# One copy of q and k in DRAM, read back by strided loads

## The reference

```
q, k, v = x @ Wq.T + bq, x @ Wk.T + bk, x @ Wv.T + bv        # per head 512 x 16
p = softmax(q k^T / sqrt(512)), then p * triu(ones)          # mask after the softmax
a = layernorm(x + p v) * gamma + beta
x2 = layernorm(x + a)
h = silu(x2 W1^T s1) * (x2 W2^T s2)                          # 1024 wide
h = gelu(h H1^T t1); h = gelu(h H2^T t2); y = h W3^T s3
out = layernorm(x2 + y)
```

## Time and profile before

| | us |
|---|---|
| median of 3 runs | 1239.02 |
| lowest and highest | 1238.99, 1242.73 |
| the profiled execution | 1233.03 |
| its span, from the first to the last instruction | 1231.2 |
| PE busy in the span | 1169.1 (95%) |
| mean granted clock of PE | 0.973 of full |
| DMA traffic | 128.48 MB, mean 104 GB/s |

### The profile page before, as it was taken

The page is one execution under the profiler, slowest core; times in us unless marked ns, Lnnn a source line. Parts: engine busy times, 40 slices in busy tenths (PEclk is TensorE's granted clock), DMA queues, the critical chain, the costliest instruction groups (busy, mean ns, idle before and its releaser), DMA issues.

```text
span 1231.2 us, 18365 instructions
## 1 busy us (share of the span) xinstructions
PE 1169.1 (95%) x7430; PEld 815.6 (66%) x7430; DVE 785.5 (64%) x1135; ACT 526.2 (43%) x698; POOL 590.7 (48%) x502
## 2 busy tenths in 40 slices
PE   4379999999999999999999999999999999999997
PEld 2134777758776677857777587766778577775886
DVE  3657677477646686477774777466864777748412
ACT  5777411564127621375115641276213751155310
POOL 5867532465235642376324652355423763246432
PEclk8569999999999999999999999999999999999999
DMA  9973631425334343246414263343432454141000
GB/s 339 285 197 67 190 86 36 123 70 172 70 88 105 138 103 70 53 105 187 87 36 122 64 178 70 88 106 137 103 71 53 105 181 89 41 96 46 1 1 18
DMA packets 55451, 128.48 MB, mean 104 GB/s; under 512 B 4032, under 2 KB 15680, under 8 KB 53312
## 3 DMA queue, kind: packets, MB, share of 16 engines
q1 hardware_dynamic: 51008, 115.44, 36.5%
q10 hardware_dynamic: 4352, 11.80, 2.9%
HBM read 88.95 MB, written 38.27 MB: 103 GB/s over the span
## 4 chain that ended last, share of the span: by engine, by line
PE 87%; POOL 4%; DMA 4%; issue 3%; ACT 1%; DVE 1%; POOLq 0%; ACTq 0%; SPq 0%; DVEq 0%
PE PS L1018 51%; PE PS L935 9%; PE PS L954 6%; PE PS L903 6%; PE PS L855 5%; PE PS L1104 3%; PE PS L961 3%; PE PS L872 2%; PE PS L967 2%; DMA raw_weights<-h2T_dram 1%; POOL raw_weights L520 1%; POOL diag_probs L453 1%; DMA x_tok<-x_dram 1%; DMA raw_weights<-h1T_dram 1%; DVE out_tok L711 1%
## 5 line engine op out<-in xcount | busy, mean ns | idle before, releaser
L665 DVE TENSOR_REDUCE neg_max<-PS 128x3 f32<-128x1536 f32 x168 | 257.6, 1575 | 61.1 <-PE PS L903 61.1
L440 POOL TENSOR_TENSOR hidA_lo<-hidA_full,hidA_hi 128x512 fp32r<-128x512 f32 x128 | 174.1, 1360 | 244.7 <-DVE hidA_hi L822 186.8
L575 ACT ACTIVATE probsT<-PS 128x1024 f32<-128x1024 f32 x256 | 248.0, 1021 | 76.8 <-PE PS L935 76.7
L1018 PE MATMUL PS<-hidA_hi,g 128*128 128x512 f32 x512 | 205.7, 402 | 0.0
L1018 PE MATMUL PS<-hidC_hi,g 128*128 128x512 f32 x512 | 204.1, 399 | 0.0
L1018 PE MATMUL PS<-hidA_lo,g 128*128 128x512 f32 x512 | 200.1, 391 | 0.0
L1018 PE MATMUL PS<-hidC_lo,g 128*128 128x512 f32 x512 | 200.0, 391 | 0.0
L453 POOL TENSOR_TENSOR diag_probs<-probsT,mask 128x512 f32<-128x512 f32 x120 | 157.3, 1315 | 57.4 <-PE PS L1018 31.1
L440 POOL TENSOR_TENSOR hidC_lo<-hidC_full,hidC_hi 128x512 fp32r<-128x512 f32 x64 | 82.3, 1286 | 194.5 <-DVE hidC_hi L822 194.5
L935 PE MATMUL PS<-stacks 66*128 66x512 f32 x512 | 152.3, 419 | 0.2 <-ACT probsT L575 0.2
L596 ACT ACTIVATE hidC_full<-PS,scales 128x512 f32<-128x512 f32 x64 | 44.1, 690 | 239.3 <-PE PS L1018 239.3
(11 more groups left out here) (106 smaller groups left out, 1805.3 us busy)
## 6 DMA issues: line engine op xcount, KB each, us to landing
stacks<-qk_rows SPq DMA_DIRECT2D x64, 512.0 KB
stacks<-qk_rows SPq DMA_DIRECT2D x32, 1024.0 KB
qk_rows<-qk_hi SPq DMA_DIRECT2D x32, 512.0 KB, 3.7
qk_rows<-qk_lo SPq DMA_DIRECT2D x32, 512.0 KB, 5.6
xT_sb<-xT_dram SPq DMA_DIRECT2D x8, 512.0 KB, 4.0
raw_weights<-h1T_dram ACTq DMA_DIRECT2D x8, 512.0 KB, 9.8
raw_weights<-h2T_dram ACTq DMA_DIRECT2D x8, 512.0 KB, 8.3
x_tok<-x_dram SPq DMA_DIRECT2D x8, 512.0 KB, 5.7
```

What stands on the lines that cost most here:

```text
L440: nc.gpsimd.tensor_tensor(lo[:, m, :], full[:, m, :], hi[:, m, :], ALU.subtract).then_inc(lo_done, 1)
L575: nc.scalar.activation(PT[:, s % RING, 2 * pair:2 * pair + 2, :], PS[:, 2 * pair:2 * pair + 2, :], ACT.Exp, scale=SCALE).then_inc(exp_done, 1)
L665: nc.vector.tensor_reduce(NEGM[:, group // 2, at + lo:at + hi], PS[:, 3 * side:3 * side + hi - lo, :], AX.X, ALU.max, negate=True).then_in ...
L1018: ins = nc.tensor.matmul(out, d if swapped else w, w if swapped else d, start=(k == 0 and part == 0), stop=(k == kts - 1 and part == 1))
```

## The change

`qk_rows` holds q and k once. Its axes are now q or k, group, side (which half of the four heads), dimension, hi or lo, and two heads x 512, so one row is 4 KB: both heads of a side for one dimension and one part. The weights' columns are put into another order on the host (`pairs_outside`), so that a tile's partitions are group, side, dimension, and the tile is the head of the pair. Four stores of 512 KB remain.

The rows of a stack become: partition 4d + 2 (q's part) + (k's part), plus 64 per side in the loads for the row scores. q's rows, being wanted twice, are loaded with a partition stride of 2 by two DMAs; each of k's parts is loaded with a stride of 4 by two DMAs. A load for the row scores is 2 DMAs of 64 rows and 4 of 32, over all 128 partitions; a transposed load is 2 of 32 rows and 4 of 16, over partitions 0 to 63, and the one of the maxima. In `ST` the q values of the four heads now lie ahead of the k values. The counts on the semaphores follow. Loading, rounding and testing the weights stay.

```diff
--- before.py
+++ after.py
@@ -104,7 +104,7 @@
 
     XT = place("xT_sb", [P, DT, S], F32)
     ZB = place("z_blocks", [P, HD, 2 * HD], F32)
-    ST, ST_f = both("stacks", [P, 2, QUAD, 2, S])
+    ST, ST_f = both("stacks", [P, 2, 2, QUAD, S])
     VXT = place("v_ones", [P, QT * VX + HD], F32)
     X = place("x_tok", [P, QT, D], F32)
     Vm = place("v_negative", [P, QT, D], F32, top[0])
@@ -139,7 +139,7 @@
     UNBOUNDED = place("scores_unbounded", [1, 1], I32)
     assert top[0] <= nc.sbuf_usable_end, top[0] - nc.sbuf_usable_end
 
-    qk_rows = nc.dram_tensor("qk_rows", [4, D, 2, S], F32, kind="Internal").ap()
+    qk_rows = nc.dram_tensor("qk_rows", [2, NQUAD, 2, HD, 2, 2 * S], F32, kind="Internal").ap()
     max_rows = nc.dram_tensor("max_rows_d", [2, H * QT * P], F32, kind="Internal").ap()
 
     with ExitStack() as ctx:
@@ -205,7 +205,7 @@
             if value > 0:
                 engine.wait_ge(s, value)
 
-        LOADS_S, LOADS_T = 32, 32
+        LOADS_S, LOADS_T = 6 * 16, 7 * 16
         IN_PER_BATCH = 2 * LOADS_S + 2 * LOADS_T
 
         def after_stack(engine, b, group, transposed):
@@ -283,6 +283,15 @@
             sp.dma_start(ID[:], ident).then_inc(consts_in, 16)
             for t, src in ((GAM, gamma), (BET, beta), (S3, s3)):
                 sp.dma_start(t[:], src.rearrange("(a d) -> a d", a=1).to_broadcast([P, D])).then_inc(consts_in, 16)
+
+            def load_rows(stack, group, landed):
+
+                for r1 in range(2):
+                    sp.dma_start(stack(slice(r1, P, 2))[:, 0:2, :].rearrange("m pair s -> m (pair s)"),
+                                 qk_rows[0, group].rearrange("side d part e -> (side d part) e")).then_inc(landed, 16)
+                    for r2 in range(2):
+                        sp.dma_start(stack(slice(2 * r1 + r2, P, 4))[:, 2:4, :].rearrange("m pair s -> m (pair s)"),
+                                     qk_rows[1, group, :, :, r2, :].rearrange("side d e -> (side d) e")).then_inc(landed, 16)
 
             def load_stacks(b, group, transposed):
 
@@ -298,31 +307,33 @@
                 else:
                     after(sp, scoredT, b, n, back)
                 if group == 0 and not transposed:
-                    after(sp, rows_stored, b, 8 * 16, 8 * 16)
-                rows = qk_rows.rearrange("r (d h) a s -> (r d) h a s", d=HD)
+                    after(sp, rows_stored, b, 4 * 16, 4 * 16)
                 if not transposed:
-                    for side in range(2):
-                        heads = group * QUAD + 2 * side
-                        sp.dma_start(ST_f[side * SPLIT:(side + 1) * SPLIT, group % 2, :, 0, :],
-                                     rows[:, heads:heads + 2, :, :].rearrange("p h a s -> p (h a) s")).then_inc(
+                    load_rows(lambda rows: ST_f[rows, group % 2, 0, :, :], group, stack_in[group % 2])
+                else:
+                    for r2 in range(2):
+                        sp.dma_start(ST_f[r2:SPLIT:2, group % 2, 0, :, :].rearrange("m (side pair) s -> m side (pair s)", pair=2),
+                                     qk_rows[0, group].rearrange("side d part e -> (d part) side e")).then_inc(
                                          stack_in[group % 2], 16)
-                else:
-                    sp.dma_start(ST_f[0:SPLIT, group % 2, :, :, :],
-                                 rows[:, group * QUAD:(group + 1) * QUAD, :, :]).then_inc(stack_in[group % 2], 16)
+                    for r1 in range(2):
+                        for r2 in range(2):
+                            sp.dma_start(ST_f[2 * r1 + r2:SPLIT:4, group % 2, 1, :, :].rearrange(
+                                "d (side pair) s -> d side (pair s)", pair=2),
+                                         qk_rows[1, group, :, :, r2, :].rearrange("side d e -> d side e")).then_inc(
+                                             stack_in[group % 2], 16)
                     if group % 2 == 0:
                         after(sp, max_stored, b, 32, 16 * (group // 2 + 1))
-                    sp.dma_start(ST_f[SPLIT:ROWS, group % 2, :, 0, :],
+                    sp.dma_start(ST_f[SPLIT:ROWS, group % 2, 0, :, :],
                                  max_rows[:, group * QUAD * S:(group + 1) * QUAD * S].rearrange(
                                      "r (h s) -> r h s", h=QUAD)).then_inc(stack_in[group % 2], 16)
 
             def store_rows(b):
 
-                for part, done, products in ((QKhi_f, qk_biased, ((0, 1), (0, 2))), (QKlo_f, qk_split, ((2, 3), (1, 3)))):
+                for part, values, done in ((0, QKhi_f, qk_biased), (1, QKlo_f, qk_split)):
                     for a in range(2):
                         after(sp, done, b, 2 * DT, (a + 1) * DT)
-                        for r in products[a]:
-                            sp.dma_start(qk_rows[r, :, a, :].rearrange("(t p) s -> p t s", p=P),
-                                         part[:, a * DT:(a + 1) * DT, :]).then_inc(rows_stored, 16)
+                        sp.dma_start(qk_rows[a].rearrange("g side d part (pair s) -> part (g side d) pair s", pair=2)[part],
+                                     values[:, a * DT:(a + 1) * DT, :]).then_inc(rows_stored, 16)
 
             def chunks(b, first, count, source):
 
@@ -420,7 +431,7 @@
             sp.wait_ge(out_ready, QT * B)
             sp.dma_start(out[(B - 1) * S:B * S, :].rearrange("(t p) d -> p t d", p=P), OUT[:]).then_inc(out_stored, 16)
             sp.wait_ge(out_stored, 16 * B)
-            sp.wait_ge(rows_stored, 8 * 16 * B)
+            sp.wait_ge(rows_stored, 4 * 16 * B)
             sp.wait_ge(max_stored, 2 * 16 * B)
 
 
@@ -624,7 +635,7 @@
         @block.vector
         def _(dve):
             nc.vector.memset(ONESF[:], 1.0).then_inc(consts_set, 1)
-            nc.vector.memset(ST_f[SPLIT:ROWS, :, :, 1, :], 1.0).then_inc(consts_set, 1)
+            nc.vector.memset(ST_f[SPLIT:ROWS, :, 1, :, :], 1.0).then_inc(consts_set, 1)
             nc.vector.memset(VXT[:], 1.0).then_inc(consts_set, 1)
             nc.vector.memset(NEGM[:], 0.0).then_inc(consts_set, 1)
             nc.vector.memset(HALF[:], -0.5).then_inc(consts_set, 1)
@@ -802,7 +813,7 @@
                         after(dve, qk_split, b, 2 * DT, 4 * DT)
                     if m == 4 and not last:
                         sum_squares(b + 1)
-                        after(dve, rows_stored, b, 8 * 16, 16 * 16)
+                        after(dve, rows_stored, b, 4 * 16, 8 * 16)
                     nc.vector.scalar_tensor_tensor(out=hidA_full[:, m, :], in0=PS[:, bank1(m, 1), :],
                                                    scalar=SC[:, 1, m:m + 1], in1=SIL[:, m % 2, :],
                                                    op0=ALU.mult, op1=ALU.mult).then_inc(up_done, 1)
@@ -901,8 +912,8 @@
                     for side in range(2):
                         rows = slice(side * SPLIT, (side + 1) * SPLIT)
                         ins = nc.tensor.matmul(PS[:, base + apart * side + n, :],
-                                               ST[rows, group % 2, 2 * pair, 0, qt * P:(qt + 1) * P],
-                                               ST[rows, group % 2, 2 * pair + 1, 0, :],
+                                               ST[rows, group % 2, 0, pair, qt * P:(qt + 1) * P],
+                                               ST[rows, group % 2, 0, 2 + pair, :],
                                                start=True, stop=True)
                 ins.then_inc(scored, 1)
 
@@ -932,8 +943,8 @@
                         after(pe, max_split, b, 2, 2)
                         after_units(pe, maxed, b, 2 * units_of(b), 2)
                     for j in (2 * pair, 2 * pair + 1):
-                        ins = nc.tensor.matmul(PS[:, j, :], ST[0:ROWS, g % 2, j, 1, kt * P:(kt + 1) * P],
-                                               ST[0:ROWS, g % 2, j, 0, :], start=True, stop=True)
+                        ins = nc.tensor.matmul(PS[:, j, :], ST[0:ROWS, g % 2, 1, j, kt * P:(kt + 1) * P],
+                                               ST[0:ROWS, g % 2, 0, j, :], start=True, stop=True)
                     ins.then_inc(scoredT, 1)
 
             def values(b, s):
@@ -1163,10 +1174,10 @@
     def turned(w):
         return np.ascontiguousarray(np.asarray(w).T)
 
-    def dim_major(w):
+    def pairs_outside(w):
 
         w = np.asarray(w)
-        return w.reshape(H, HD, *w.shape[1:]).swapaxes(0, 1).reshape(w.shape)
+        return np.moveaxis(w.reshape(NQUAD, 2, 2, HD, *w.shape[1:]), 2, 0).reshape(w.shape)
 
     def by_partition(*vectors):
 
@@ -1175,8 +1186,8 @@
     arrays = {
         "x": np.ascontiguousarray(x.reshape(B * S, D)),
         "xT": np.ascontiguousarray(x.transpose(0, 2, 1).reshape(B * D, S)),
-        "wqT": turned(dim_major(L0_attn_Wq)), "wkT": turned(dim_major(L0_attn_Wk)), "wvT": turned(L0_attn_Wv),
-        "bqk": by_partition(dim_major(L0_attn_bq), dim_major(L0_attn_bk)), "bv": np.asarray(L0_attn_bv),
```

(2 more changed lines are left out.)

## The result

Ten runs of each kernel on one chip: 1230.41 us with the change (1227.12 to 1233.33), 1238.84 us before (1235.11 to 1242.73). The ratio, taken between runs made next to each other, is 0.9941, interval 0.9921 to 0.996: **7.3 us faster, with about 2.4 us either way** (the two medians alone differ by 8.4). Forecast were 1234.3 us and a gain of 4.7. The profiled executions differ by less: 1229.9 against 1233.03 us, a gain of 3.1 (span 1228.2 against 1231.2). Written to DRAM were 21.50 MB instead of 38.27.

A forecast was written before the change was run, and what follows sets the result against it. The first 82 us were taken as bound by weight starvation (7.1 us) and row maxima, PE as full later. -7.1 + 0.9 stall + 1.5 clock = -4.7 took 1239.0 to 1234.3 us, range 1228.5 to 1240.

The forecast's parts named there:

- Stores, 5.3 us: Startup, batch 0: halving the stores lets the first stack load leave SP at 22.5 us, 5.3 us earlier.
- The rate of strided loads, 380 to 400 GB/s: Row-score loads: strided over all 128 partitions, they move 380 to 400 GB/s, within possible bounds of 217 and 407.
- rival 1: Row-score loads: strided loads stay at the half rate, only the stores' part helps; gain 2.1, 1236.9 us; chance 0.22.
- The weights, 7.1 us of starvation gone, 0.9 kept: First 82 us: late weight pieces cost 7.1 us, which goes; 0.9 us of stall stays beside group 0's transposed load.
- The clock, 1.5 us: Startup, PE idle from about 73 to 75.5 us: its lowered clock costs 1.5 us, bounds 0 and 2.5.
- The startup's sum, -4.7 us: Startup: -7.1 weight starvation + 0.9 stall + 1.5 clock loss = -4.7 us, bounds -7.1 and -2.1.
- x_tok being late in each batch: Later batches, kernel before: five more late x_tok at 1.1 us explain nearly all of the median's 6 us above the profile.
- x_tok and the transposed loads, 0 us: SP queue, group 2: seven issues instead of one just fit before x_tok; cost 0, bounds -2.3 and +9.5 us.
- the sign that I had named for rival 3: SP queue: x_tok's issue held up by SP's own issues, listed among the signs that the forecast is wrong.
- rival 3: SP's queue behind the group 2 load: x_tok late in every batch, +4.8 us, 1243.8 us; chance 0.13.
- Rival 2: Startup and late batches: the whole gain comes and x is relieved, -7.1 - 2.3 = -9.4, 1229.6 us; chance 0.15.

The follow-up runs named there:

- experiment 7: Changed kernel with each q and k store issued twice, the second time into a spare array (eight stores again): 1231.44 us, ratio 0.9949.
- Experiments 8 and 9: Changed kernel, each row-score load cut in two, reaching 64 partitions (8, by side) or all 128 (9, by parity): 1238.04 and 1230.8 us.
- by parity: Experiment 9: changed kernel, twelve row-score DMAs a group, each over all 128 partitions with strides of 4 and 8: 1230.8 us, ratio 0.9949.
- experiments 7 and 11: 7: changed kernel, every store issued twice, 1231.44 us; 11: changed kernel, w3T pieces third among the weights instead of last, 1232.06 us.
- experiment 10: Changed kernel with sixteen instead of two clock-keeping matmuls on PE before the first exp: 1229.08 us, ratio 0.9944.
- x early: Experiments 5 and 6: x_tok loaded into its own buffer ahead of the group 2 load; kernel before 1232.07 us, changed kernel 1225.22 us.
- loads by side: Experiment 8: changed kernel, twelve row-score DMAs a group, each over 64 partitions: 1238.04 us, ratio 0.9998.
- experiments 1 and 2: Only the first two batches computed, the other six left out: kernel before 372.03 us, changed kernel 369.64 us.

## Why the prediction was right, and where it was not

The time fell into the range in part by luck: two errors of opposite sign met in it, as the sum below shows.

**Stores, 5.3 us: right.** The first load came at 22.39 for a forecast of 22.5, and experiment 7 gave 5.8 us back.

**The rate of strided loads, 380 to 400 GB/s: right**, 400 in SP's own queue. It was the disputed step, with rival 1 on its other side. Experiments 8 and 9 have the same number of DMAs with equally few rows in each, and differ in the partitions that a DMA reaches: 235 GB/s over 64, 290 over 128. The Trainium skill, in "SBUF — State Buffer", section "Door 1: The DMA port swizzle", has the rate go by the ports that a transfer's partitions reach. Strides of 2 and 4 over 128 partitions at 400 GB/s against 231 to 235 over 64 agree with it. By its formula a stride of 8, which half of the bytes by parity have, reaches eight of the 16 ports again; half at 400 and half at 231 would give 293 GB/s, an estimate from that page and these rows, and measured were 290. No run separates the stride of 8 from the smaller DMAs. The Trainium skill has a rule to coalesce small transfers ("DMA: Bandwidth & Descriptors", section "Rules for kernel authors"); going against it cost no time here: 512 KB DMAs became 256 and 128 KB, and even 128 and 64 KB in experiment 9, and 1230.8 us stood beside 1230.41.

**The weights, 7.1 us of starvation gone, 0.9 kept: mechanism right, the rest mis-sized.** The median piece of h1T lands 5.8 us after its issue instead of 9.8, and h1T and h2T are never waited for. (The prediction misread one row: the piece of 9.99 us was issued at 34.80 and landed at 44.79. Nothing in the sum hangs on it.) But the stall that I kept for the transposed load, 0.9 us, is 2.1 us at POOL and 2.7 at ScalarE; experiments 7 and 11 point to that load. The maxima ended 1.2 us later than forecast, at 71.75, since the first ones started at 31.47 and not at 29 to 30: PE took up the first group at 30.2, and I had it landed at 28.3. The first exp came 4.5 us earlier, not 6.2: POOL's stall is 1.2 us above the 0.9, and the pieces' work itself ran 0.4 us later (29.04 instead of 28.61). My upper bound for that stall was 2.5 us: the size should have been taken from the earlier trace rows, where the same overlap had left POOL idle for 2.50 us, and nothing in the change touches that load's reach. This and the clock are the two terms that were mis-sized.

**The clock, 1.5 us: mechanism right, size too small.** It took 3.1 us between the first exp and the stores of batch 1, 2.4 of which experiment 10 gets back. I had sized it from the earlier trace rows, where half clock lasts some 3 us behind an idle time of about 2.4 us; here PE was idle for 4.17 us and the half clock lasted from 76 us to past 86. One row of another gap was too little to size it by.

**The startup's sum, -4.7 us.** In the profiled pair it is -4.5 + 3.1 = -1.4, and -2.7 with the clock's fall of the old kernel at 126 us. The timed runs give 2.4 by the two batches and 6.85 by the pair with x early, with some 2 and 4 us of uncertainty. The traces say why the profiled pair can be low. In the seven other profiled executions that keep four stores and row-score loads over all 128 partitions, the first exp starts between 74.52 and 77.69, in six of them at 76.36 or later. Of the old startup, it was 81.65 in the execution that I predicted from, and 82.56 and 83.77 in two others; with the loads by side 82.88. The one I had was the best of these, so a gain worked out from it is small against that of the median. That is read from few traces. The forecast came within 3.9 us of the time with two errors of opposite sign: too large a gain against its own profile (by 1.6), too small a one against the timed runs (by 2.6).

**Where the old kernel's 6 us above its profile are.** I put nearly all on x_tok being late in each batch. That step was wrong. x early gives 5.9 us in the median, but the profiled execution had nearly all of that loss itself: from the stores of batch 2 to the end of the span it took 1231.2 - 273.41 = 957.8 us, and 1226.7 - 274.00 = 952.7 with x early, 5.1 us less. The two late batches are only part of it; the other periods are 0.2 us longer than 143.24 as well, and the last batch 1.7. So x accounts for about 0.8 of the 5.8 us between profile and median. The rest lies in other differences between executions ("What stays open", below).

**x_tok and the transposed loads, 0 us: right, in another way.** I had the seven issues at 0.45 us, 3.2 together. SP's queue in batch 1:

```profile
233.45 1.24 SPq L315 DMA_DIRECT2D stacks<-qk_rows  x2
234.72 2.50 SPq L320 DMA_DIRECT2D stacks<-qk_rows  x4
237.27 0.44 SPq L326 DMA_DIRECT2D stacks<-max_rows_d  x1
237.75 1.02 SPq L408 DMA_DIRECT2D x_tok<-x_dram  x1
```

and its DMA issues by line (ns, least, median, most), beside the earlier trace rows:

```profile
L293 SPq DMA_DIRECT2D stacks<-qk_rows x128: 448/596/1221, 23.0 to 1039.6; - x128
L320 SPq DMA_DIRECT2D stacks<-qk_rows x128: 557/593/607, 59.6 to 1107.3; - x128
L290 SPq DMA_DIRECT2D stacks<-qk_rows x64: 456/592/1549, 22.4 to 1038.3; - x64
L315 SPq DMA_DIRECT2D stacks<-qk_rows x64: 592/601/1436, 58.3 to 1104.8; - x64
```

An issue of the transposed load costs 0.59 to 0.60 us, and all seven with x behind them 4.3 us. So x_tok leaves at 237.75, 0.44 us after VectorE's last output tile (237.31) and held by SP itself: the sign that I had named for rival 3. It didn't matter, because x waits for the data ahead of it, not for its issue. From the first issue of the group 2 load to the landing of x it is 9.64 us in the mean of seven batches before and 9.68 after. With the change x was late twice, in the last two batches, where it landed 10.0 and 10.6 us after that issue. The rows of the last one (landed at 1105.3):

```profile
1099.54 0.41 SPq L408 DMA_DIRECT2D x_tok<-x_dram  x1
...
1105.33 1.01 DVE L731 TENSOR_TENSOR z<-z,x_tok 128x256 f32<-128x256 f32 x1 [2.78 <-DMA x_tok<-x_dram]
...
1109.31 0.42 PE L965 MATMUL PS<-probsT,ones_col 128*32 128x128 f32 x8 [0.51 <-POOL diag_probs L464]
```

Rival 3's price, 1.3 us per late batch, was about right (0.8 to 1.4 in these two traces), its condition was not: 0.14 us more per issue didn't move the landing. Rival 2's relief did not come either: x early is worth as much with the change as without.

**What stays open.** Why the time varies from one execution of a kernel to the next is shown in part: it goes with the clock. In the three groups of experiments the kernel before ran 64 times. The eleven executions with a mean granted clock of 0.975 took 1232.60 to 1234.73 us, and the ten with 0.968 or less took 1239.75 to 1245.74. The trace with loads by side, of 1239.33 us, shows such a stretch: half clock from 86 to past 90 us, and 48.3 us from the first exp to the stores of batch 1, against 44.3 to 44.8 in the three traces of old loads with eight batches. What decides in an execution whether the clock falls isn't shown. Nor do the half-rate loads explain the spread: by parity it is 11.9 us, as wide as by side (11.1). Whether the change's timed 7.3 us lie wholly in the startup isn't settled either: the pair of experiments 1 and 2 leaves up to 5 us for the later batches, the pair of 5 and 6 less than 1, and their intervals overlap.

## What to carry to other kernels

Look at GB/s beside the DMA share: full engines at half the rate meant here a transfer that reaches half of the partitions, and a stride over all of them got the rate back although it cost three times as many DMAs. When two chains end together and one is shortened, look at what TensorE does in the new gap: here the clock took 2.4 to 3.1 of 4.5 us. And a transfer that was awaited on an edge gained by being moved ahead of the large load it queued behind (5.2 to 5.9 us over the run); 0.4 us more of issues in front of it had not moved its landing.

## What the runs showed of the hardware

- Row-score loads over 128 partitions with a stride of 2 or 4 moved 400 GB/s of their own share of the DMA engines (30 to 36 us); with strides of 4 and 8, in DMAs of half the size, it was 290; over 64 partitions at a time 231 and 235.
- An issue on SP costs 0.59 to 0.60 us for a strided load of 128 or 256 KB and 0.45 us for the one of 1 MB of the earlier trace rows: it doesn't go by the bytes.
- After 4.17 us of idle time PE ran at 1.2 instead of 2.4 GHz from 76 us until past 86, though busy without a gap from 80 us on. At the end of attention 0 its clock fell in 8 of the 11 profiled executions with 2.3 to 2.6 us of idle time and in none of the three with 2.05 to 2.11 us; the stretch from the stores of batch 1 to the gate layers was about 1.8 us longer with the fall (15.0 to 15.4 us against 13.2 to 13.6).
- Half-rate loads of one queue slow another's transfers: the median h1T piece took 9.8 us to land before and 8.8 beside loads by side, and 5.8 and 5.3 us beside loads over all partitions (six and twelve DMAs).
